# Windowed attention over 4x4 image tiles: the tiles paired in the array's rows, and the DMA mask for v replaced by ScalarE

## The reference, cut to what matters

```
x0  = groupnorm(x, 32 groups)
qkv = 1x1 convolution of x0 with qkv_w            # 3*128 channels, 32 heads of 8
msq = concat([qkv, avg_pool5(qkv)])               # full and pooled, inside each window
q, k = relu(q), relu(k);  v = [v, 1]
kv  = einsum('nld,nlm->ndm', k, v)                # per window and head: 8 x 9
out = einsum('nld,ndm->nlm', q, kv);  out = out[:-1] / (out[-1:] + 1e-15)
y   = batchnorm(1x1 convolution of out with proj_w)
result = x + y
```

## Time and profile before

| what | value |
|---|---|
| median of 3 runs | 886.46 us (883.51 to 887.85) |
| profiled execution: its own time / its span | 883.81 us / 882.0 us |
| granted TensorE clock | 0.999 of full speed |
| TensorE matmul (PE), busy | 845.7 us, 96% |
| TensorE weight load (PEld), busy | 688.9 us, 78% |
| VectorE (DVE), busy | 700.7 us, 79% |
| GpSimd (POOL), busy | 658.6 us, 75% |
| ScalarE (ACT), busy | 481.2 us, 55% |
| hardware DMA queue | 20.1% of 16 engines' time, 59.5 MB |

### The profile page before, as it was taken

How to read it: one execution, slowest core, us unless ns; L and a number is a source line. 1 busy time by engine, 2 the same in 40 slices (tenths; PEclk the granted TensorE clock), 3 DMA queues, 4 the chain that set the end, 5 groups by cost and what they waited for, 6 DMA issues and landing times.

```text
span 882.0 us, 63773 instructions
## 1 busy us (share of the span) xinstructions
PE 845.7 (96%) x28322; PEld 688.9 (78%) x28322; DVE 700.7 (79%) x1252; ACT 481.2 (55%) x1349; POOL 658.6 (75%) x1624
## 2 busy tenths in 40 slices
PE   0789999999999999999999999999999999999997
PEld 0568888888888888888888888888888888888885
DVE  7758888887778888898777888888777777777776
ACT  0346565656555555556565656555656464656563
POOL 2568787878787878777777778787878787878781
PEclk9999999999999999999999999999999999999999
DMA  6122322111122323111113232211111111111111
GB/s 237 41 77 87 98 88 79 49 47 48 48 83 84 103 84 100 50 45 51 44 52 97 88 103 84 86 46 50 48 48 48 48 48 48 48 48 48 47 49 47
DMA packets 39081, 60.06 MB, mean 68 GB/s; under 512 B 8560, under 2 KB 33648, under 8 KB 39024
## 3 DMA queue, kind: packets, MB, share of 16 engines
q1 hardware_dynamic: 39024, 59.52, 20.1%
HBM read 19.38 MB, written 18.87 MB: 43 GB/s over the span
## 4 chain that ended last, share of the span: by engine, by line
PE 94%; DVE 3%; issue 1%; DMA 1%; SPq 0%; ACT 0%; DVEq 0%
PE ps L705 24%; PE ps L689 17%; PE ps L661 14%; PE ps L670 9%; PE ps L677 9%; PE ps L786 7%; PE ps L777 6%; PE ps L790 4%; PE ps L678 4%; DVE stats L455 1%; DMA x_all<-x 0%; DVE kvc_full L563 0%; DVE kvc_pool L563 0%; DMA vm_full<-v_full 0%; DVE kvc_full L511 0%
## 5 line engine op out<-in xcount | busy, mean ns | idle before, releaser
L366 ACT ACTIVATE vm_pool<-ps,cst 128x256 f32<-128x256 f32 x576 | 230.1, 479 | 0.0
L376 ACT ACTIVATE q_full<-ps 128x384 f32<-128x384 f32 x96 | 47.2, 491 | 274.1 <-PE ps L677 274.1
L563 DVE TENSOR_TENSOR kvc_full<-ps,cst 128x864 f32<-128x864 f32 x192 | 193.1, 1047 | 4.4 <-PE ps L689 4.4
L563 DVE TENSOR_TENSOR kvc_pool<-ps,cst 128x864 f32<-128x864 f32 x192 | 193.0, 1046 | 0.5 <-PE ps L689 0.5
L286 POOL TENSOR_TENSOR xd<-x_all,mean_t 128x384 f32<-128x384 f32 x95 | 78.6, 827 | 152.1 <-PE ps L678 135.8
L661 PE MATMUL ps<-wkv_sb,xn 128*128 128x256 f32 x576 | 141.4, 382 | 22.9 <-DVE xn L519 22.9
L264 POOL TENSOR_TENSOR x_all<-y_pool,x_all 128x96 f32<-128x96 f32 x380 | 148.8, 425 | 13.2 <-ACT y_pool L405 13.2
L661 PEld LDWEIGHTS ps<-wkv_sb,xn 128*128 128x128 f32 x576 | 109.4, 191 | 33.0 <-issue 22.9
L705 PEld LDWEIGHTS ps<-kvc_full,q_full 64*32 64x32 f32 x9216 | 108.6, 105 | 26.0 <-issue 26.0
L292 POOL TENSOR_TENSOR xn<-xd,rstd_t 128x96 f32<-128x96 f32 x380 | 121.8, 367 | 8.1 <-DVE xn L519 0.7
L705 PE MATMUL ps<-kvc_full,q_full 64*32 64x72 f32 x9216 | 125.3, 230 | 0.6 <-DVE kvc_pool L563 0.6
(11 more groups left out here) (74 smaller groups left out, 1315.1 us busy)
## 6 DMA issues: line engine op xcount, KB each, us to landing
vm_full<-v_full SPq DMA_DIRECT2D x384, 54.0 KB, 1.9
out<-x_all SPq DMA_DIRECT2D x96, 192.0 KB, 1.9
x_all<-x SPq DMA_DIRECT2D x36, 384.0 KB, 3.5
x_all<-x SPq DMA_DIRECT2D x6, 768.0 KB, 7.8
cst<-consts SPq DMA_DIRECT2D x1, 170.0 KB, 11.0
wkv_sb<-wkv SPq DMA_DIRECT2D x1, 128.0 KB, 10.9
o_sb<-proj SPq DMA_DIRECT2D x1, 128.0 KB, 10.1
wq_sb<-wq SPq DMA_DIRECT2D x1, 64.0 KB, 10.6
```

The lines of the kernel that those rows point to most:

```text
L366: last = act.activation(heads[:, e, :, :, 0:D], src, ACT.Copy, scale=col(C_VP + e))
L563: last = dve.tensor_tensor(kvc[:, g], src.to_broadcast(shape), own, ALU.mult)
```

## The change

Windows are taken in **pairs**, and each of the two has a slot of 32 rows. For the out products all 128 rows are contracted at once (128x32 tiles), so that each pair needs one matmul where two were added before: q is written twice, once per slot, with a scale column that is 1 in the rows of that slot and 0 elsewhere, and the zeros do the separating. For the kv products k is written twice (mask by slot) into 64-column blocks, and v once per pair (2 full copies, 3 pooled ones, in place of 4 and 6). The tiles are 64x64. v of the full windows is masked by ScalarE, and the DMAs of `spread_v` are gone. `conv_q` computes the even and the odd windows of the pairs in separate matmuls with weights of their own. TensorE's order of stages stays.

```diff
@@ sizes
-EF = QG * WF
-EP = QG * WP
+PAIR = 2
+EF = QG * WF // PAIR
+EP = QG * WP // PAIR
@@ buffers and banks
-        q_full = sb("q_full", [TF * 4, WF, Q4 + PX])
-        q_pool = sb("q_pool", [TP * 4, WP, Q4 + PXP])
+        QS = G * PAIR * PX
+        q_full = sb("q_full", [QS // 2 + (HALF + 1) * QS])
+        q_pool = sb("q_pool", [QG_AT + (HALF + 1) * QD])
-        KVF, OUTP, KVP, OUTF = 0, 2, 4, 4
-        OUTF_LAST = 6
+        KVF, KVP = 0, 4
+        OUTF, OUTF_LAST, OUTP = 5, 6, 7
-        Q_F, Q_P = 7, 6
+        Q_F, Q_P = 6, 7
@@ sync
-            def spread_v(s):
...
-                    spread_v(s + 1)
@@ gpsimd (the views of xn and xp are laid out by pairs; three memsets go)
-            pool.memset(q_full[:], 0.0).then_inc(pads_zero, 1)
-            pool.memset(vm_full[:], 0.0).then_inc(pads_zero, 1)
-            pool.memset(v_full[:], 1.0).then_inc(pads_zero, 1)
@@ scalar
+            def masked_k(k, src, masks):
+                src = src.rearrange("p t (j g c) -> p t j g c", j=QG, g=G)
+                slots = k[:].rearrange("p t (j z c) -> p t j z c", j=QG, c=Q4)
+                act.activation(slots[:, :, :, 0:4:3], src, ACT.Relu, scale=col(masks))
+                return act.activation(slots[:, :, :, 1:3], src, ACT.Relu, scale=col(masks + 1))
             def relu_k(s):
-                act.activation(k_full[:], kv_tiles(KV_F, TF)[:, :, 0:P], ACT.Relu).then_inc(km_f, 1)
+                masked_k(k_full, kv_tiles(KV_F, TF)[:, :, 0:P], C_KF).then_inc(km_f, 1)
...
-            def copy_v(s):
...
+            def masked_v(vm, src, pairs, masks):
+                heads = vm[:].rearrange("p e t (h c) -> p e t h c", c=HC)
+                src = src.rearrange("p t (h m) -> p t h m", m=D)
+                for e in range(pairs):
+                    last = act.activation(heads[:, e, :, :, 0:D], src, ACT.Copy, scale=col(masks + e))
+                return last
+            def masked_v_full(s):
                 act.wait_ge(conv_f, s + 1)
-                wait(act, vm_f, 16 * EF * s)
+                wait(act, kv_f, s)
+                masked_v(vm_full, kv_tiles(KV_F, TF)[:, :, P:], EF, C_VF).then_inc(vm_f, 1)
@@ relu_q (relu_q_pooled likewise, with 216 and 234 values)
+                def copy(at, first, pairs, slot):
+                    to = q_full[:, at:at + pairs * QS].rearrange("p (n k j) -> p k n j", k=4, j=PX)[:, 0:4:3]
+                    src = ps[:, Q_F, first:first + 2 * pairs * PX].rearrange("p (x n j) -> p x n j", x=2, j=PX)
+                    return act.activation(to, src, ACT.Relu, scale=col(C_SLOT + slot))
+                copy(QS, PX, HALF, 0)
+                copy(QS // 2, 0, HALF + 1, 1).then_inc(qm_f, 1)
@@ ScalarE's order
-                    copy_v(s + 1)
+                    masked_v_full(s + 1)
...
                     relu_k_pooled(s + 1)
-                    masked_v_pooled(s + 1, None if is_first(s) else s - 1)
-                elif not is_first(s):
+                if not is_first(s):
                     copy_y_pooled(s - 1)
+                if not is_last(s):
+                    masked_v_pooled(s + 1)
@@ tensor, conv_q
-                pe.matmul(ps[:, Q_F, 0:SP], wq_sb[:], xn[:, p], start=True, stop=True).then_inc(q_f, 1)
+                full = xn[:, p].rearrange("p (g x a r) -> p r g a x", x=PX, a=EF, r=PAIR)
+                pooled = xp[:, p].rearrange("p (q j) -> p q j", j=H64)[:, :, 0:WIN_H * PXP].rearrange(
+                    "p q (a r x) -> p r q a x", r=PAIR, x=PXP)
+                for r in range(PAIR):
+                    last = pe.matmul(ps[:, Q_F, PX + r * SP // PAIR:PX + (r + 1) * SP // PAIR], wq_sb[:, r], full[:, r],
+                                     start=True, stop=True)
+                last.then_inc(q_f, 1)
+                wait(pe, num_p, s)
+                for r in range(PAIR):
+                    last = pe.matmul(ps[:, Q_P, PXP + r * SPP // PAIR:PXP + (r + 1) * SPP // PAIR], wq_sb[:, r], pooled[:, r],
                                     start=True, stop=True)
+                last.then_inc(q_p, 1)
@@ kv_tile (n = EF * KC or EP * KC, now 72 and 108)
-                for r in range(G):
-                    for i in range(4):
-                        last = pe.matmul(ps[Q4 * i:Q4 * (i + 1), bank + r, t * n:(t + 1) * n],
+                for g in range(G):
+                    for j in range(QG):
+                        for r in range(2):
+                            last = pe.matmul(ps[H64 * j:H64 * (j + 1), bank + r, (t * G + g) * n:(t * G + g + 1) * n],
+                                             k[rows, t, at:at + H64], vm[rows, :, t, i * KC:(i + 1) * KC],
@@ out products (n = 72)
-            def out_tile(pooled, t, e, full_bank=OUTF):
+            def out_tile(t, g, full_bank):
+                for c in range(4):
+                    r, e = c // EF, c % EF
+                    q = QS + (4 * t + c) * QS + g * Q4
+                    last = pe.matmul(ps[Q4 * c:Q4 * (c + 1), full_bank, at:at + n], q_full[:, q:q + Q4],
+                                     kvc_full[:, r, (t * G + g) * EF + e], start=True, stop=True)
+            def out_tile_of_pooled(t, g, z):
+                for c in range(4):
+                    last = pe.matmul(ps[Q4 * c:Q4 * (c + 1), OUTP, at:at + n], q_pool[:, q:q + Q4],
+                                     kvc_pool[:, r, (t * G + g) * EP + c % 2 + z], start=z == 0, stop=z == 1)
@@ waits on TensorE
-                pe.wait_ge(vm_f, 16 * EF * (s + 1))
-                wait(pe, y_copied, s - 1)
+                    pe.wait_ge(y_copied, s - 1)
@@ project: out_wait(s + 1), on kvc_p, moves from ahead of L786 to ahead of L790;
@@ the wait on km_f ahead of L790 goes
```

More of the change, by code:

```diff
@@ L35 @@
 C_OWN = P
-C_VP = C_OWN + QG * KC
+C_VF = C_OWN + QG * KC
+C_KF = C_VF + EF
+C_VP = C_KF + PAIR
 C_TP = C_VP + EP
-C_PACK = C_TP + EP
+C_KP = C_TP + EP
+C_SLOT = C_KP + PAIR
+C_SLOT_P = C_SLOT + PAIR
+C_PACK = C_SLOT_P + PAIR
 N_CONST = C_PACK + P
@@ L75, in build @@
     HALF = NW // 2
-    assert HALF * KC <= 512 and TF * EF == HALF and TP * EP == HALF
+    assert HALF * KC <= 512 and TF * G * EF == HALF and TP * G * EP == HALF
+    assert WIN_H * PXP <= H64 and QG_AT + Q4 * 2 + PXP * 2 <= QD + Q4
     FOURS = SPB // 4
@@ L348, in relu_k_pooled, with masked_v_pooled @@
                 wait(act, kv_p, s)
-                act.activation(k_pool[:], kv_tiles(KV_P, TP)[:, :, 0:P],
-                               ACT.Relu, scale=1 / 25.0).then_inc(km_p, 1)
-            def copy_v(s):
-                act.wait_ge(conv_f, s + 1)
-                wait(act, vm_f, 16 * EF * s)
[L355 to L359, removed]
+                masked_k(k_pool, kv_tiles(KV_P, TP)[:, :, 0:P], C_KP).then_inc(km_p, 1)
+            def masked_v(vm, src, pairs, masks):
[5 more added lines that the diff above has]
+            def masked_v_full(s):
+                act.wait_ge(conv_f, s + 1)
+                wait(act, kv_f, s)
+                masked_v(vm_full, kv_tiles(KV_F, TF)[:, :, P:], EF, C_VF).then_inc(vm_f, 1)
+            def masked_v_pooled(s):
                 act.wait_ge(conv_p, s + 1)
                 wait(act, kv_p, s)
[L363 to L369, removed]
+                masked_v(vm_pool, kv_tiles(KV_P, TP)[:, :, P:], EP, C_VP).then_inc(vm_p, 1)
             def relu_q(s):
@@ L383, in relu_q_pooled, with copy @@
                 wait(act, out_p, s)
-                act.activation(q_pool[:, :, :, 0:PXP],
-                               ps[:, Q_P, 0:SPP].rearrange("p (n e j) -> p n e j", e=WP, j=PXP),
-                               ACT.Relu, scale=1 / 25.0).then_inc(qm_p, 1)
+                def copy(at, first, pairs, slot):
+                    to = q_pool[:, at:at + pairs * QD].rearrange("p (n d) -> p n d", d=QD)[:, :, 0:3 * Q4].rearrange(
+                        "p n (k c) -> p k n c", c=Q4)[:, 0:3:2, :, 0:PXP]
+                    src = ps[:, Q_P, first:first + 2 * pairs * PXP].rearrange("p (x n j) -> p x n j", x=2, j=PXP)
+                    return act.activation(to, src, ACT.Relu, scale=col(C_SLOT_P + slot))
+                copy(QD, PXP, HALF, 0)
+                copy(QG_AT, 0, HALF + 1, 1).then_inc(qm_p, 1)
             def to_image(s):
@@ L639, in _ @@
             dve.tensor_scalar(proj_sb, proj_sb, bn_inv[:], None, ALU.mult).then_inc(proj_scaled, 1)
+            for e in range(EF):
+                ones = vm_full[:, e].rearrange("p t (h c) -> p t h c", c=HC)[:, :, :, D]
+                dve.tensor_copy(ones, col(C_VF + e).unsqueeze(2).to_broadcast(list(ones.shape)))
             for e in range(EP):
@@ L656, in conv_kv @@
                 pe.wait_ge(xn_ready, s + 1)
-                wait(pe, num_p, s - 1)
+                if isinstance(s, int) and s == 1:
+                    pe.wait_ge(vm_f, 1)
+                    pe.wait_ge(km_f, 1)
                 for t in range(TF):
@@ L692, in kv_tile @@
-                return last
-            def out_tile(pooled, t, e, full_bank=OUTF):
-                q, kvc, bank, wins = (
```

(36 more changed lines are left out.)

149 lines of the change are left out of this document (79 added, 70 removed).

## The result

The changed kernel takes **961.08 us** (960.25 to 962.57, 4 runs); the kernel before took 885.1 us beside it. The ratio is 1.086 (95% interval 1.082 to 1.089): slower by 76 us, where 902 us and a range of 852 to 935 were forecast. Rival C, the strided read, had 962.

The account below looks back on a forecast made before the run. TensorE was taken as the bound, with ScalarE's chain ahead of project. Strip: 4.26 + 1.12 + 1.94 + 1.60 = 8.92 us against 8.74; +0.18 times 94 = +17 on 883.81, plus 1: 902 us, range 852 to 935.

Parts of the forecast that it names:

- Rival C: conv_q full on TensorE takes twice its 0.65 us through the strided read: 9.57 us a strip, 962 us; chance 0.11.
- The moving operand is now read every fourth float: conv_q full on TensorE: strided read costed at nothing; lower bound nothing, upper bound a doubling of the 0.65 us.
- Out products: TensorE's out stage: 112 records on 4 tiles, paced by columns, 1.94 us where it was 2.16: -0.22 us a strip.
- rival B: Out stage paced by instructions, records under 14.0 ns apart: -0.31 us a strip, 855 us; chance 0.19.
- D: Rival: out products' weight loads don't lie under matmuls of the same tile: 0.76 us more a strip, 972 us; chance 0.08.
- kv products: TensorE's kv stage: same number of records, half the columns and tiles, 1.60 us where it was 1.64: -0.04 us.
- conv_q: TensorE: pooled part's 4 records each need their own weight load, 0.44 us for 0.36: +0.08 us a strip.
- ScalarE: Its q and v copies, costed at 0.33 to 0.49 us each, delay o_sb; project begins at 4.26 us instead of 3.84.
- Covered: Remaining ScalarE copies, VectorE and GpSimd work were expected to stay hidden; kv products' waits had 0.8 us of cover.
- The set-up and the first strips: Extra VectorE set-up and fewer memsets, once each and below 1 us, left at nothing; all 94 strips costed alike.
- 1 had been added for the median: Whole time: the profiled 883.81 us lies 0.3% below the median of 886.46, so 901 became 902 us.

Follow-up runs that it names:

- Experiment 1: Changed kernel with xn laid out so a window's 16 values lie side by side and conv_q reads contiguously (the contiguous variant): 895.76 us, ratio 1.012.
- experiment 2: Kernel before with conv_q full reading xn every fourth float, ScalarE then reading PSUM contiguously: 946.66 us, ratio 1.071.
- experiments 4: Changed kernel with xn read contiguously, and to_image and pooled_out put ahead of both masked v copies on ScalarE: 878.92 us, ratio 0.993.
- Experiment 5: Changed kernel with xn read contiguously, and ScalarE's order v copy 0, to_image, pooled_out, v copy 1: 858.34 us, ratio 0.970.

## Why the prediction was wrong

The sum was 17 us, the measured 76. The step that failed is one: "The moving operand is now read every fourth float ... I take nothing". It measured 0.67 us a strip (0.76 to 1.43), just above the upper bound of 0.65 that was written beside it, and with it the strip is 8.92 + 0.67 = 9.59 of the measured 9.62. Experiment 1 takes it away and gets 65 us back; experiment 2 puts it into the kernel before and pays 63. That rival was set out with the right price and then given 0.11. (That its 962 us lies within 1 us of the measured time is luck in part: its strip of 9.57 was 0.05 too short, 5 us in all, and the rest of the sum 6 us too high, as below.) The reason was a poor row: ScalarE's read of PSUM, another engine on another memory, was let stand for TensorE's read of SBUF. The rule of the Trainium skill that rival C names spoke about just this access, and no row spoke against it. With no row of the same engine on the same memory, the two ends of the bound should have shared the chance about evenly, and the range had to hold the upper one.

The other steps, by the contiguous variant, where only they are left (895.8 us against 902, 8.93 us a strip against 8.92):

- *Out products*, -0.22: right, -0.27 (1.89 us, in the changed kernel 451.44 to 453.33). 28 rounds on four tiles; the full part's 12 rounds take 0.77 us (452.21 - 451.44), 0.064 each where the columns make 0.0625, or 16 ns a record. So columns decide, not instructions, and rival B, which needs less than 14, is out. So is D: were the loads open, the stage would take 2.7 us. The Trainium skill's statement ("TensorE: Matmul & The Clock Gate", Part 3) that a load overlaps a running matmul only in other row groups does not hold here, where each tile has all rows and a round with its load takes no more than 0.064 us.
- *kv products*, -0.04: +0.01. The full part is 0.80 us where 12 rounds of 0.0625 make 0.75; what the 0.05 are wasn't tried.
- *conv_q* pooled, +0.08: right, 0.43 us in place of 0.36 (445.36 - 444.93).
- *ScalarE*: right in place and size. The full copies were costed at 0.467 and 0.49 each, and lie so; the pooled q at 0.33 and 0.34, but the pair took 0.77 or 0.78. That cost nothing, because it fills the 0.11 us that ScalarE was to wait for `conv_kv`: v starts 2.70 us after `conv_q`, where 2.69 was forecast. The load of `project` was forecast to start at 4.15 and starts at 4.18 (448.35 - 444.17); experiments 4 and 5 show that this order is worth 37 us, more than the out products gain (0.27 x 94 = 25).
- *Covered*: `copy_y_pooled`, VectorE and GpSimd didn't show, as said.
- *The set-up and the first strips*, costed at nothing and like all others: up to the fourth `conv_q` the contiguous variant takes 60.3 us and the kernel before 63.5. Of these 3 us 0.9 lie ahead of the first `conv_q` (31.45 and 32.32). Most of the rest is one stretch in each of the next two strips in which TensorE stands still and the profile shows nothing that it waits for: 1.74 and 1.98 us before, 0.47 and 0.56 in the contiguous variant. So 3 of the 6 us by which 902 was too high are explained; why these stretches are shorter wasn't tried. Another 1.4 come from the strips: over the 92 behind the fourth start the mean is 8.93 us against 8.76 before, which one strip had as 8.74, so they differ by 0.165 where 0.18 was forecast. And 1 had been added for the median.

So without the read the sign was right and the size near (12 us slower where 17 was forecast), and it would still have been a loss of 1%: the change saves TensorE 0.26 us a strip in the two kinds of products and loses more than that through the copies of v, which ScalarE makes just ahead of the one for which TensorE waits. Experiment 5 moves a single copy out of the way and makes of the loss a gain of 3%.

## What to carry to other kernels

When an edit changes the layout of what TensorE streams, count the 16-byte lines that the moving operand touches. Here, with float32, the matmul slowed down in proportion below two values from each line, to half pace at one. An engine that is half idle can still set the time: look at what it does between the event that starts it and the result that another waits for, and put there only what must be there. One copy of v in the gap ahead of `to_image` and one behind left TensorE no wait here; both ahead cost 37 us, both behind 21 (experiments 1, 4 and 5).

## What the runs showed of the hardware

- TensorE's moving float32 operand: 0.83 to 0.90 ns a value with two or more values from each 16-byte line, 1.7 ns a line with fewer, for steps of 12, 16 and 32 bytes alike. In the profile's groups the record of 192 columns of the changed kernel lasts 536 ns on the mean,

```profile
L723 PE MATMUL ps<-xn,wq_sb 128*128 128x192 f32 x384 | 154.3, 536 | 0.0
```

against 352 with the values side by side,

```profile
L723 PE MATMUL ps<-xn,wq_sb 128*128 128x192 f32 x384 | 88.1, 352 | 0.0
```

and both count as busy. The busy share of TensorE, 96% and 95%, doesn't tell a slow read from work.

- One sum of GpSimd depends on the layout of xn too: that of two columns of each window (`ht`) lasts 0.55 us when it walks xn in steps of 64 bytes (changed kernel), 0.54 in steps of 32 (every second float) and 0.36 in steps of 16 (contiguous). The next sum, which adds one column of xn to it, lasts 0.44 us in all three. TensorE doesn't wait for either, so neither shows in the time.
